# GpSimd's waits for its own landed gathers at every twelfth chunk: a five-layer graph network on one Trainium2 core

## The reference, cut to what matters

```python
edge_index = jnp.stack([src, dst])
x = _layernorm(x + _L0_gnn_ref(x, L0_gnn_W, L0_gnn_b, src, dst))       # segment_sum of (x @ W)[src] * coef
x = _layernorm(x + _L1_gnn_ref(x, edge_index, edge_attr_32, ...))      # two times:
#   msg = x[src] @ W_msg + edge_attr @ W_edge; agg = segment_max(msg, dst); leaky_relu(agg + x @ W_root + b)
x = _layernorm(x + _L2_gnn_ref(x, src, dst, L2_gnn_W, L2_gnn_b))       # segment softmax of relu(x[src]), weighted sum
x = _layernorm(x + _L3_gnn_ref(x, L3_gnn_W, ..., edge_index))          # attention over neighbours, with self loops
```

## Time and profile before

| what | value |
|---|---|
| time, median of 2 runs | 4265.42 us (4257.02 and 4273.81) |
| span of the profiled execution | 4261.0 us |
| TensorE's mean granted clock in it | 0.659 of full |
| busy share PE, DVE, ACT, POOL | 45%, 66%, 44%, 64% |
| indirect transfers of GpSimd | about 2,700 |
| HBM read and written over the span | 230.36 MB and 291.54 MB |

### The profile page before, as it was taken

The page is one execution under the profiler, slowest core; times in us unless marked ns, Lnnn a source line. Parts: engine busy times, 40 slices in busy tenths (PEclk is TensorE's granted clock), DMA queues, the critical chain, the costliest instruction groups (busy, mean ns, idle before and its releaser), DMA issues. The chain is left out here.

```text
span 4261.0 us, 39832 instructions
## 1 busy us (share of the span) xinstructions
PE 1919.8 (45%) x8382; PEld 1417.5 (33%) x8382; DVE 2819.2 (66%) x10490; ACT 1859.7 (44%) x3815; POOL 2740.4 (64%) x2760
## 2 busy tenths in 40 slices
PE   5578634777766666644444357777710000000000
PEld 2244103666654554522222157777700000000000
DVE  8899854777765655568878767777655545454545
ACT  8699102656642222224444446565632323232323
POOL 7366656666646666656666466666457666676766
PEclk9899556877778777766666556666655555555555
DMA  1111764555545555545566444444322222222221
GB/s 51 49 35 36 213 203 111 145 135 138 143 122 178 181 173 177 179 139 181 180 187 185 145 135 164 152 157 158 125 77 72 65 72 68 68 69 67 72 65 51
DMA packets 380540, 524.65 MB, mean 123 GB/s; under 512 B 221914, under 2 KB 255983, under 8 KB 380042
## 3 DMA queue, kind: packets, MB, share of 16 engines
q1 hardware_dynamic: 286154, 366.89, 26.1%
q0 software_dynamic: 94144, 155.21, 15.4%
HBM read 230.36 MB, written 291.54 MB: 122 GB/s over the span
## 5 line engine op out<-in xcount | busy, mean ns | idle before, releaser
L1632 POOL DMA_INDIRECT l_G<-t,src x391 | 415.0, 1061 | 228.3 <-issue 104.6
L1949 POOL DMA_INDIRECT out<-O,nidx x392 | 393.4, 1004 | 229.3 <-issue 110.9
L1311 POOL DMA_INDIRECT l1a_G<-t,src x391 | 376.5, 963 | 232.1 <-issue 111.7
L2167 PE MATMUL l_psR<-l_diag,l_ones 128*128 128x128 f32 x2 | 0.8, 501 | 1131.2 <-DVE l_diag L2031 1131.2
L1932 POOL DMA_INDIRECT l_G<-t,src x391 | 403.2, 1031 | 166.7 <-issue 118.2
L1311 POOL DMA_INDIRECT l1b_G<-t,src x391 | 380.2, 972 | 197.7 <-issue 110.4
L642 POOL DMA_INDIRECT O<-x_pad,nidx x344 | 326.7, 950 | 188.9 <-DMA O<-x_pad,nidx 97.0
L975 POOL DMA_INDIRECT l_G<-xs,src x327 | 310.3, 949 | 169.0 <-issue 88.4
L2167 PEld LDWEIGHTS l_psR<-l_diag,l_ones 128*128 128x128 f32 x2 | 0.5, 310 | 1131.3 <-DVE l_diag L2031 1131.3
L207 ACT ACTIVATE O<-O,l_shift,l_rstd 128x96 f32<-128x96 f32 x784 | 291.2, 453 | 27.2 <-DVE l_shift L201 27.2
L1989 DVE TENSOR_TENSOR l_e<-l_G,l_to_score 128x8 f32<-128x8 f32 (+3 forms) x51 | 8.5, 166 | 444.2 <-DMA l_G<-t,src 444.2
(11 more groups left out here) (350 smaller groups left out, 6554.5 us busy)
## 6 DMA issues: line engine op xcount, KB each, us to landing
h<-l_G SPq DMA_DIRECT2D x96, 392.0 KB, 2.4
t<-l1b_t_out SPq DMA_DIRECT2D x48, 768.0 KB
h<-l_G SPq DMA_DIRECT2D x48, 768.0 KB, 3.8
xs<-en_y SPq DMA_DIRECT2D x48, 392.0 KB, 3.7
t<-l_t_out SPq DMA_DIRECT2D x48, 392.0 KB
l_H<-t SPq DMA_DIRECT2D x48, 392.0 KB, 3.2
en_y<-x_pad SPq DMA_DIRECT2D x48, 384.0 KB, 4.9
t<-l_tr_out SPq DMA_DIRECT2D x48, 384.0 KB
```

Source lines behind the costliest of these rows:

```text
L1311: pool.indirect_dma_start(tile(c)[:, q, :], None, table, bass.IndirectOffsetOnAxis(k.src[:, at:at + 1], 0))\
L1632: pool.indirect_dma_start(tile(c)[:, q, :], None, table, bass.IndirectOffsetOnAxis(k.src[:, at:at + 1], 0))\
L1949: pool.indirect_dma_start(out, bass.IndirectOffsetOnAxis(k.nidx[:, at:at + 1], 0), k.O[:, at, :], None, bounds_check=NP - 1, oob_is_err=Fa ...
```

## The change

A constant `TURN = 12` is added. The landing wait stays only at chunks whose number is a multiple of 12. In `entry`, where it used to bound the number of chunks that count on the same one of eight semaphores, a wait for the chunk eight back takes its place at the other chunks from 8 on. In `layer3` it stays ahead of every sixth scatter. No transfer and no instruction of another engine is added, removed or moved, and the slot waits and the wait for `normed` stay.

```diff
@@ entry @@
             for c in range(LATE):
-                if c >= 1:
+                if c and c % TURN == 0:
                     pool.wait_ge(placed[(c - 1) % RING], 128 * ((c - 1) // RING + 1))
+                elif c >= RING:
+                    pool.wait_ge(placed[c % RING], 128 * (c // RING))
@@ layer0 @@
-                if RAW < c < NCH:
+                if RAW < c < NCH and c % TURN == 0:
                     pool.wait_ge(gathered.of(c - 1), gathered.by(c - 1))
@@ layer1 @@
-                if c and c < NCH and c % 2 == 0:
+                if c and c < NCH and c % TURN == 0:
                     pool.wait_ge(gathered.of(c - 1), gathered.by(c - 1))
@@ layer2 @@
-                if 1 <= c < NCH:
+                if 1 <= c < NCH and c % TURN == 0:
                     pool.wait_ge(gathered.of(c - 1), gathered.by(c - 1))
@@ layer3, scatter(c) @@
-                if c + 2 < NCH:
+                if c + 2 < NCH and c % (TURN // 2) == 0:
                     pool.wait_ge(gathered.of(c + 2), gathered.by(c + 2))
                 pool.wait_ge(normed, c + 1)
```

More of the change, by code:

```diff
@@ L33 @@
 MSG_EPS = 1e-7
+TURN = 12
 LEAK = 0.01
```

## The result

The changed kernel takes 3888.45 us (median of 2 runs, 3885.73 to 3891.17) against 4265.42 us. The ratio is 0.9111, with a 95% interval of 0.9084 to 0.9137. The prediction was 3877 us in a range of 3845 to 3965: right, with 11 us of the gain missing. The profiled execution has a span of 3889.4 us, 371.6 us less than before, and it tells where each of them came from.

A forecast was written before the change was run, and what follows sets the result against it. POOL was taken to set the pace of all five layers, and its landing waits to give back 61 + 68 + 49 + 74 + 81 + 65 = 398 us, less 10 for longer transfers: 4265.4 - 388 = 3877 us, range 3845 to 3965.

The forecast's parts named there:

- Entry gives only what the others leave: Entry: 78 us of POOL's waits go, but the barrier waits for SyncE's stores, so 65 us come back.
- the 13 us of cover: Entry: the wait put in costs nothing; if it held, under 2 us a chunk, 34 times, lies under 13 us.
- Layer 0, 61 us: Layer 0: 36 of 40 landing waits go, each giving back 1.69 us, 61 us in all.
- Layers 1a and 1b, 68 and 49 us: 20 of 24 waits go in each, at 3.39 and 2.45 us; 1b's DVE period of 10.07 fits under POOL's 10.2.
- the term for longer transfers: All stages: POOL without waits meets about 15% more DVE instructions, lengthening transfers by 0 to 20 us, taken as 10.
- Layer 2, 74 us: Layer 2: 44 of 48 waits go at 1.69 us each; POOL's 10.9 us a chunk stays above DVE's 9.7.
- rival 1: Other engines become the bound in layers 0, 1b and 2, losing 92 us: 3969 us; chance 0.18.
- The prediction's sign of it: POOL's waits on PE, DVE or a chunk's store growing past 20 us in a layer would show the forecast wrong.
- Layer 3, 81 us: Layer 3: of 47 scatters with the wait 8 keep it, 39 go at 2.07 us each, 81 us.
- Slots: Gathers run at most three to four chunks ahead; DVE stays two chunks away from holding POOL up; nothing taken off.
- Rival 2: Long runs of transfers are slow, up to 1253 ns each in all seven groups: 4553 us; chance 0.05.
- Rival 3: The edit does nothing, since slot waits for an earlier chunk fall due at the same moment: 4265 us; chance 0.04.

The follow-up runs named there:

- the kernel with the late numbering: Changed kernel, but POOL's 64 gathers in `numbering` wait until DVE has done its sums: 3964.82 us (one run).
- layer 2 alone: Kernel before, with landing waits only at every 12th chunk in layer 2 and nothing else changed: 4200.09 us, ratio 0.9861.
- the new order: Layer 2: PE multiplies chunk t-4 before it mixes chunk t-1; in the changed kernel 3848.3 us, in the kernel before 4266.81 us (ratio 0.9999).
- the halved product: Changed kernel, PE multiplying only every second tile in layer 2's last product for chunks 2 to 47: 3866.56 us, ratio 0.9063.

## Why the prediction was right, point by point

- **POOL sets the pace, and a removed wait gives back its idle time less the gap.** Right, and shown by the dose: 3949, 3888, 3859 and 3845 us at every 6th, 12th, 24th chunk and never (ratios 0.9255, 0.9111, 0.9062, 0.9013). The exception is layer 2, below.
- **Entry gives only what the others leave.** Right in kind. The size was off: 65 us forecast, 73.8 measured. The step that failed is "the block gives back only 671.3 - 606.1": it took the end of POOL's last transfer for the end of POOL's part. POOL's way out of the block takes 8.15 us more, and that was hidden too. 678.9 - 606.1 = 73 us is the right difference of the same rows. The 73.8 came in part from a long execution: over all of them the gain is 69 to 74 us. The waits put in stand at 32 chunks and not 34, and their price, had they held, would have been up to 64 us and not under the 13 us of cover; what was right is that they cost nothing, with POOL's last transfer at 593.32 us as forecast.
- **Layer 0, 61 us; measured 52.6.** The four waits kept, at chunks 12, 24, 36 and 48, are 3.30, 3.63, 5.49 and 2.89 us long, 15.3 us in all and not 4 x 1.99. The mean of 40 waits was taken for each of the four, but most of the 40 came in step with SyncE's stores and were near 1.8 us. Now the waits fall beside the stores: at 952 to 954 us SyncE issues three of them, and the wait of 5.49 us begins right behind, at 955. That cause is only read from the timeline.
- **Layers 1a and 1b, 68 and 49 us; measured 63.0 and 45.3.** In 1a transfers got 4.7 us longer in all in this execution, which is in the term for longer transfers. In an execution of the same layer code, in the kernel with the late numbering, they are as short as before (376.3 us in all) and the layer is 525.5 us, so the 5 us that are missing there lie within the spread of executions. In 1b the kept waits are 14.4 us where 11 were counted. Layer 1b was called safe "by a hair". It held at every 12th chunk, and even with no waits POOL isn't held up in it.
- **Layer 2, 74 us; measured 63.1.** This is where a step failed: "Layer 2 ... 9.7 us a chunk against 10.9". The 9.7 was DVE's period without its waits for gathers. It says nothing of a loop that runs through PE and ACT, in which the others wait for each other while DVE waits for a gather. That loop takes 11.5 us at the granted clock of 0.52 in the round shown, 11.1 us a chunk over the layer, against 10.3 for POOL, and it became the bound: rival 1, in one of its three layers. The experiments with layer 2 alone, the new order on both kernels and the halved product show it. The prediction's sign of it did show, under another name: the 149.8 us of "issue" hold 34 us beyond the plain gaps, past the 20 us that it named.
- **Layer 3, 81 us; measured 74.2.** The eight waits kept are as forecast (18.9 us). Its transfers got longer by 4.2 and 5.5 us, and the 1153.6 us it is measured from are the shortest of four executions.
- **Longer transfers, 10 us between 0 and 20.** Outside layer 2 busy time rose by 16 us (4.7, 1.6, 4.2, 5.5 and 1.0, less 0.8), inside it fell by 29 us. So the upper end was the nearer one for the layers that POOL bounds: 16 us, where the prediction had 20 by the rule of the Trainium skill ("SBUF — State Buffer", section "SBUF: two separate sides") in full. Why layer 2's transfers got shorter, 1061 to 987 ns, can be counted in the two traces. Before, 44 of the 391 transfers begin inside DVE's tensor_tensor of the earlier trace rows and take 1.53 us in the mean, and 144 begin inside its chain (L1660, 1.06 us). After, 36 and 106 do, and take 1.24 and 0.97 us. So fewer meet DVE and those that do meet it lose less: DVE now waits for ACT (53.9 us in 49 times, 12.1 in 11 before) where it waited for the landing. Transfers that begin inside the equally long tensor_tensor with the product in PSUM (L1689) are not longer, 945 ns in 46. "About 15% more of such meetings" was thus wrong for this layer.
- **Slots.** The text ahead of the prediction says four slots in every layer. Layer 2 has three (`SLOTS = 3` in its code). In the changed kernel 21 of POOL's 24 held-up starts in layer 2 ("issue" over 0.4 us) are at a chunk's first transfer, where the slot waits stand. A fourth slot wasn't tried, so how much it would hide of the loop is open. No number of the forecast rested on the fourth.
- **Rival 2 (long runs are slow)** fell at 96, 192 and up to 391 transfers, with few of them under way at once (5 at most in entry), and its one sign, 1253 ns in `numbering`, has another cause. **Rival 3** fell.
- **The total.** 398 - 10 = 388 us forecast, 377 measured. The stages add up to 372 us: the five layers gave 35 us less than counted (8 + 5 + 4 + 11 + 7) and entry 9 us more, and 10 of the 26 us between the two were in the term for longer transfers. The medians differ by 5 us more than the spans of the two profiled executions (371.6).

## What to carry to other kernels

A wait that stands behind work just issued costs its own idle time less the gap that is there anyway, and only where its engine sets the pace. Before giving such waits up in a prediction, time each closed loop of the other engines from the timeline (a step to the same step of the next round, following what released it): an engine's period less its waits is no measure of a loop. And try an order again once the bound has moved: the one in layer 2 was worth 0 us beside the old waits and 32 to 45 us without them (by the ratios, and by the layer's length).

## What the runs showed of the hardware

- GpSimd issued up to 391 indirect transfers in a row without waiting for a landing, at 948 to 1044 ns each, the same as in runs of eight. In entry without landing waits a gather landed after 2.5 us (median), and at most 5 were under way at once, so no deep queue was ever there to be seen.
- GpSimd needs 8.15 us from the end of its last transfer to its next one when it comes last to the barrier after entry (at 607.0 us with waits at every 6th chunk, at 671.3 us before); its DRAIN at the barrier ends 7.25 us after that transfer. Where the other engines come last, as in the changed kernel, DVE starts again at 605.53 us, 2.06 us after its own last instruction.
- 64 transfers in a row took 1253 ns each beside DVE and ACT at work, and 951 ns beside idle ones. Long ones (over 1.4 us, 23 of the 64 in the changed kernel) all began inside a tensor_tensor of DVE; ACT's work beside a transfer did not lengthen it. In layer 2 a tensor_tensor of DVE on two tiles of SBUF lengthened the transfers that began inside it to 1.53 us in the mean (44 of them), and one of the same length with a PSUM input left them at 0.945 us (46).
- In layer 2 the mean granted clock is higher with the new order in both kernels: 0.61 and 0.70 in the changed one, 0.62 and 0.67 in the one before, where the time stayed the same.
